# First attention of a two-layer decoder: another sequence of the work within a step

## The reference

```python
q = input_embeds @ Wq.T + bq
k = input_embeds @ Wk.T + bk
v = input_embeds @ Wv.T + bv
q, k, v = (split_heads(q), split_heads(k), split_heads(v))
q, k = _apply_rope(q, k)
scores = jnp.einsum('bhqd,bhkd->bhqk', q, k) * scale
attn = jax.nn.softmax(scores, axis=-1)
out = jnp.einsum('bhqk,bhkd->bhqd', attn, v)
return out.reshape(B, S, NUM_HEADS * HEAD_SIZE) @ Wo.T + bo
...
x = _layernorm(x + _L0_attn_ref(x, ...), axis=-1)
```

## Time and profile before

| | |
|---|---|
| median of 3 runs | 2269.36 us (2264.51 to 2286.98) |
| the profiled execution: time, span | 2269.79 us, 2268.0 us |
| PE busy over the span | 2008.5 us (89%) |
| DVE busy | 1494.7 us (66%) |
| ACT busy | 1108.4 us (49%) |
| POOL busy | 683.0 us (30%) |
| the first attention's steps | about 57 to 380 us |

### The profile page before, as it was taken

How to read it: one execution, slowest core, us unless ns; L and a number is a source line. 1 busy time by engine, 2 the same in 40 slices (tenths; PEclk the granted TensorE clock), 3 DMA queues, 4 the chain that set the end, 5 groups by cost and what they waited for, 6 DMA issues and landing times. The chain is left out here.

```text
span 2268.0 us, 93291 instructions
## 1 busy us (share of the span) xinstructions
PE 2008.5 (89%) x41611; PEld 1429.6 (63%) x41611; DVE 1494.7 (66%) x3186; ACT 1108.4 (49%) x1913; POOL 683.0 (30%) x731
## 2 busy tenths in 40 slices
PE   4999997799877697979999999999999997988997
PEld 2666665555535584237888888788888873456446
DVE  7999984466567735777777777777777774354114
ACT  1334445466576665664455444554444543244324
POOL 5766661122132101213333333333333332001000
PEclk8999999899989999989999999999999998996999
DMA  3000000000000001000000000000000001002001
GB/s 95 3 3 3 3 3 2 6 0 0 1 3 12 0 2 32 0 1 4 4 5 4 4 4 4 5 4 4 4 4 4 4 5 52 0 1 75 1 0 38
DMA packets 34551, 22.78 MB, mean 10 GB/s; under 512 B 14857, under 2 KB 30161, under 8 KB 34194
## 3 DMA queue, kind: packets, MB, share of 16 engines
q1 hardware_dynamic: 34194, 17.38, 2.9%
HBM read 15.27 MB, written 2.10 MB: 8 GB/s over the span
## 5 line engine op out<-in xcount | busy, mean ns | idle before, releaser
L1798 PEld LDWEIGHTS psum<-dr_kq,dr_kSq 64*64 64x64 f32 x6144 | 198.4, 135 | 65.5 <-issue 55.3
L1798 PE MATMUL psum<-dr_kq,dr_kSq 64*64 64x64 f32 x6144 | 224.7, 222 | 7.6 <-POOL dr_G L2224 2.5
L2105 ACT ACTIVATE dr_Y<-psum 128x256 f32<-128x256 f32 x160 | 62.9, 393 | 313.7 <-PE psum L1804 312.7
L1798 PE MATMUL psum<-dr_GT,dr_Y 64*64 64x32 f32 x5120 | 186.8, 221 | 7.1 <-issue 6.5
L1804 PE MATMUL psum<-dr_G,dr_CT 64*64 64x32 f32 x5120 | 185.9, 222 | 1.5 <-issue 1.4
L1798 PEld LDWEIGHTS psum<-dr_GT,dr_Y 64*64 64x64 f32 x5120 | 165.9, 135 | 14.2 <-issue 9.7
L1804 PEld LDWEIGHTS psum<-dr_G,dr_CT 64*64 64x64 f32 x5120 | 166.7, 135 | 2.6 <-issue 2.5
L2194 POOL TENSOR_TENSOR dr_kSq<-dr_kSq,dr_decay 128x256 f32<-128x256 f32 x128 | 99.1, 775 | 210.5 <-PE psum L1798 207.5
L1804 PE MATMUL psum<-dr_Y,dr_GT 64*64 64x32 f32 x4096 | 147.0, 219 | 13.1 <-issue 11.3
L1804 PEld LDWEIGHTS psum<-dr_Y,dr_GT 64*64 64x64 f32 x4096 | 134.7, 135 | 37.4 <-issue 34.4
L2395 DVE COPY_PREDICATED dr_PT<-dr_level_masks,psum 128x256 f32<-128x256 uint32 x192 | 102.5, 534 | 84.2 <-PE psum L1798 81.2
(11 more groups left out here) (389 smaller groups left out, 5523.4 us busy)
## 6 DMA issues: line engine op xcount, KB each, us to landing
topk_w<-in_L_ffn_w_dram SPq DMA_DIRECT2D x16, 256.0 KB, 5.3
attn_w_x_rows<-in_x_dram SPq DMA_DIRECT2D x4, 512.0 KB, 5.4
out_dram<-store_rows SPq DMA_DIRECT2D x4, 512.0 KB, 3.6
dout_w<-in_L_attn_Wff_dram SPq DMA_DIRECT2D x3, 256.0 KB, 2.9
attn_w_rows<-in_L_attn_Wq_dram SPq DMA_DIRECT2D x1, 256.0 KB, 5.4
attn_w_rows<-in_L_attn_Wk_dram SPq DMA_DIRECT2D x1, 256.0 KB, 4.8
attn_w_rows<-in_L_attn_Wv_dram SPq DMA_DIRECT2D x1, 256.0 KB, 4.2
attn_w_rows<-in_L_attn_Wo_dram SPq DMA_DIRECT2D x1, 256.0 KB, 3.6
```

The source lines that it names most:

```text
L1798: last = nc.tensor.matmul(out(r), lhsT(r), rhs(r), start=True, stop=True)
L2105: act.activation(half_of(Y[l], l, 0), ZG[:, ZS].rearrange("p (m l) -> p m l", l=1 << l), ACT.Copy).then_inc(z_kept[l], 1)
```

## The change

No instruction is added or taken away; groups change places within a step.

- PE: the scores of t + 1 and the key projection half 0 go ahead of the output product of t - 1, scores first; the query projection half 0 of the next piece goes ahead of `pe_values`.
- DVE: the add of tile t - 1 goes behind the first rope pair of the keys.
- ACT: the exponentials of t + 1 go ahead of the copy of the heads of t.

```diff
             if t >= 1:
-                pe_out(pe, t - 1)
-            if project:
-                pe.wait_ge(turned, 6 * p + 1)
-                pe_project(pe, p, 1, 0)
             if t + 1 < NT:
                 k.hold(pe)
...
                 pe_scores(pe, t + 1)
+            if project:
+                pe.wait_ge(turned, 6 * p + 1)
+                pe_project(pe, p, 1, 0)
+            if t >= 1:
+                pe_out(pe, t - 1)
...
                     pe_v(pe, t + 1, half)
-            if t >= 0:
-                pe_values(pe, t)
             if p + 1 < NT:
                 pe.wait_ge(v_kept, 2 * t + 3)
                 pe_project(pe, p + 1, 0, 0)
+            if t >= 0:
+                pe_values(pe, t)
...
                 dve_rope(dve, p, 0, 1)
+            if p < NT:
+                dve_rope(dve, p, 1, 0)
             if t >= 1:
                 dve_add(dve, t - 1)
             if p < NT:
-                dve_rope(dve, p, 1, 0)
                 dve_rope(dve, p, 1, 1)
...
                 act_v(act, t + 1, 1)
+            if t + 1 < NT:
+                act_exp(act, t + 1)
             if t >= 0:
                 act.wait_ge(attended, t + 1)
...
                                ).then_inc(heads_ready, 1)
-            if t + 1 < NT:
-                act_exp(act, t + 1)
```

More of the change, by code:

```diff
@@ L412, in pe_step @@
                 pe_project(pe, p, 0, 1)
-            if t >= 1:
-                pe_out(pe, t - 1)
-            if project:
-                pe.wait_ge(turned, 6 * p + 1)
-                pe_project(pe, p, 1, 0)
             if t + 1 < NT:
```

## The result

The changed kernel is a little slower: 2287.8 us median of 19 runs (2278.04 to 2306.28) against 2269.3 us of 19 runs of the kernel before on the same chip. The ratio is 1.0084, with a 95% interval of 1.0062 to 1.0106: under 1%, but outside the predicted range of 2253 to 2275.

The account below looks back on a forecast made before the run. A loop through nearly full PE and DVE, each waiting once per step for the other, was taken to bound the kernel. Steady part +3.9, start +1.2, last five steps -6.3, last step -3.4 gave -4.6 us: median 2265, range 2253 to 2275.

Parts of the forecast that it names:

- The steady step: First attention, 26 intervals between transposes with a moved projection: 9.86 us each instead of 9.71, together +3.9 us.
- 0.74 scores (as 214.35 to 215.09), + 1.53 key projection: PE's step: 0.74 us from second query projection to scores, then 1.53 us from scores to key projection.
- That the DVE wait turns into an ACT wait: Query projection on PE waits 0.47 us for ACT's first value copy, starting 2.65 us after the transposes.
- Rivals A: Copy of the first value product doesn't bind, PE alone is left: step 9.40 us, median 2253 us; chance 0.15.
- B: PE has room and DVE becomes the bound: step 9.25 us, median 2249 us; chance 0.05.
- Rival C: DVE's add holds up the next transposes: slower, 2274 us with a whole add of delay; chance 0.15.
- the cover of 0.04 us: Next transposes could follow DVE's add at 9.82 us of a 9.86 us step, the thinnest cover.
- The start: First scores wait for POOL's ropes, the key projection now behind them: `max` at 64.36 instead of 63.20, +1.2 us.
- The last five steps: Steps without projections, chain through ACT: period 7.63 us instead of 9.09 with exponentials ahead of the heads copy, -6.3 us.
- The last step: Last transposes to last add at full clock: 6.7 us instead of 10.07, -3.4 us.
- rival D: Clock falls in the last step all the same: 2268 us, otherwise as forecast; chance 0.15.
- The chances: Forecast 0.50, D 0.15, A 0.15, B 0.05, C 0.15; within 1% 0.94, faster 0.03, slower 0.03.

Follow-up runs that it names:

- kernels 2: Kernel before with scores and key projection half 0 ahead of the output product, DVE's rope ahead of its add: mean step 10.25 us, last add at 394.35 us.
- kernel 5: Changed kernel with queries and keys rounded to bf16, so scores are 64 matmuls instead of 128: mean step 9.66 us, last add at 371.54 us.
- kernel 10: Changed kernel run once more without an edit: 2302.43 us against 2279.95 of the kernel before, last add at 405.95 us.
- 1: Kernel before with only the query projection half 0 moved ahead of the values: steps of 10.50 or 10.51 us, last add at 399.59 us.
- 4: Kernel before with exponentials ahead of the heads copy and DVE's rope ahead of its add, PE as before: mean step 10.90 us, last add at 403.14 us.
- kernel 7: Changed kernel with the first key projection ahead of the scores instead of behind them: mean step 10.48 us, last add at 396.34 us.
- kernel 8: Kernel before with exponentials ahead of the heads copy only from the last step with projections on: 2265.31 us, ratio to before 0.9975.
- kernel 3: Changed kernel with 16 tiny matmuls, each with its weight load, before PE's first projection: mean step 10.75 us, last add at 403.19 us.

## Why the prediction was wrong

**The steady step** was the step that failed: 3.9 us more forecast, 23.3 measured. The failing term is "0.74 scores (as 214.35 to 215.09), + 1.53 key projection". I gave each group "the spacing that rows 2 show for it", as if a spacing belonged to the group. The 1.53 us of the scores depend on what stood ahead of them: 256 instructions, right behind 128, are faster than PE's stream supplies them. In place of 1.53 the scores took 2.12 (2.18 in just the 26 intervals). That is 0.65 of the 0.79 us by which the mean interval exceeds 9.86; all other terms of the sum came within 0.06 us. The rest of the loop was right: the shortest intervals measured are 9.93.

**That the DVE wait turns into an ACT wait** was right: 25 waits for the value copy, 2.67 after the transposes for 2.65. Rivals A and B fall with it: the copy does bind, and DVE never became the bound.

**Rival C**, the add holding up the transposes, hardly showed: 2.1 us in four places, all in the last steps. In the steps with projections the transposes came 0.71 us behind the key projection for a forecast 0.65, without a wait for the add in any row, so a part of these 0.06 may be it; that isn't shown. In kernels 2 and 5 the add did hold up transposes, by 0.15 and 0.48 us in the rows shown; the cover of 0.04 us was indeed thin.

**The start** was right: the first transposes begin at 71.80 instead of 70.44, 1.4 us later for a forecast 1.2.

**The last five steps** failed, and by the same cause: 46.0 us against 45.7 before, where I had 6.3 less. Here no projections are left, and values and scores stand back to back. The changed kernel's timeline there:

```profile
371.13 0.95 PE L369 MATMUL psum<-attn_k,attn_q 32*64 32x64 f32 x68
373.69 1.10 PE L369 MATMUL psum<-attn_k,attn_q 32*64 32x64 f32 x60 [1.61 <-issue]
374.72 3.29 PE L399 MATMUL psum<-attn_heads,attn_woT 128*128 128x128 f32 x16
...
387.18 1.06 PE L379 MATMUL psum<-eye,attn_probs 128*128 128x128 f32 x8 [0.54 <-DVE X L486]
...
394.80 1.09 PE L379 MATMUL psum<-eye,attn_probs 128*128 128x128 f32 x8 [0.56 <-POOL attn_probs L518]
```

The last interval, with no scores in it, is 394.80 - 387.18 = 7.62 for a forecast 7.63. The ones with scores have 9.72, 9.16, 10.9 and 8.63. Less their stops of 1.43 and 0.97 us, the second and the fourth are 7.73 and 7.66. So the chain through ACT was right, and the stops filled what it freed. The longest, 10.9, has a stop of 1.61 us and then an output product of 3.29 us instead of 2.05.

**The last step** was right: transposes to last add 401.44 - 394.80 = 6.64 for 6.7, with clock 1.00. Windows of the changed kernel (the columns of the earlier trace rows), with the earlier trace rows to compare:

```profile
370.00:379.00 9.00, 6.85 (x213) 6.37 (x213) 2.42 (x4) 2.61 (x4) 1.90 (x1) 0.81 0.01 4
```

The clock of 0.50 that the earlier trace rows show from 370 to 379 has become 0.81 in the same window, which now holds the slow output product. In this trace the last step has the full clock and rival D falls; in the run again (10) half of it came, 1.6 us of 3.4, so this term isn't safe. Within the trace the account closes: the last add moved 21.6 us instead of -4.6, and of the 26.2 between them the steady steps are 23.3 - 3.9 = 19.4, the last five 6.6 and the start 0.2.

**The chances** were wrong where they mattered. "To be slower by that, every steady step would have to take 1 us more than I have" was true arithmetic, and the steps took 0.8 more. The time stayed within 1%, but the range ended at 2275, because it was built from waits between engines alone. None of the rivals was a cost inside one engine. The row that could have warned me is in the trace of before: its two steps of 10.43 and 10.49 us among 9.71 were those whose scores stopped after 126 and 121 matmuls for "issue". I had read only one step without such a break.

What is shown and what isn't: that the stops lie where a block of 256 instructions ends (drift, shift by 16, and the other drift in 5), that the new wait and the ACT and DVE order don't make them (1, 4), and that fewer instructions or more time between the dense groups make them fewer (5, 7). What stays open is the length of a single stop. Where the break comes late in the scores the block before it began in the values: counted back, PE went on about 2.8 to 3.8 us after it entered that block, an estimate. It doesn't explain the stops of 0.27 to 0.77 us after 17 to 37 matmuls, since the last block end before them was some 9 us back, nor those of kernel 5 after 50 matmuls or fewer, where it was over 5 us back.

## What to carry to other kernels

A group's duration in one place of the order isn't its duration in another: before moving groups within an engine, count instructions as well as time, and look at how many fall into each few us. In this kernel, two groups of many short instructions needed long ones between them. And where an order helps in one kind of step and costs in another (here the exponentials first, in the steps without projections), change it there alone: that version was 0.4% faster than the kernel before (0.05 to 0.7%).

## What the runs showed of the hardware

- PE's instruction supply can bind with nearly idle DMA engines: they were 1% busy from 60 to 400 us. The DMA view shows one instruction packet from 118.5 to 119.5 us and none from 119.5 to 122, while the scores stood still before 121.39.
- From a block's end in the values to the next in the scores PE took about 2.8 to 3.8 us for 256 instructions, counted back from the breaks. Unhindered they need some 2.3: 0.75 for the projection and the rest at the pace of the scores (1.53 us for 256), an estimate.
- Short idle times cost through the clock too, and not each time. After PE had waited 2.41 us the next group ran at half speed (clock 0.50), and after 2.47 us (kernel 8) the output product took 3.40 us instead of 2.05 (clock 0.66 from 330 to 335 us). After stops of 1.61 us (changed kernel), 1.40 and 1.70 us (kernel 10) and 1.70 us (kernel 7) the output product was slow as well (clock 0.81 to 0.86 over stretches of 9 to 12 us around it), and once in kernel 10 after a wait of 1.13 us. But after 0.97, 1.34, 1.43 and 1.56 us it kept its pace, after 1.61 us in kernels 2, 3 and 7 too, and even after 2.09 us in kernel 3. I have no run that sets these apart.
